# Graph attention kernel, phase A: one group of edges in four gets its column terms from bf16 products instead of gathers

## What is computed

```python
f1 = relu(x[row] @ nb_W[l] + nb_b[l])
f2 = relu(x[col] @ self_W[l] + self_b[l])
h = relu(concatenate([f1, f2], 1) @ att1_W[l] + att1_b[l])
log_alpha = (h @ att2_W[l] + att2_b[l])[:, 0]
mask = clip(sigmoid(log_alpha) * (ZETA - GAMMA) + GAMMA, 0.0, 1.0)
rowsum = segment_sum(mask, row) + 1e-06
d = clip(rowsum ** -0.5, 0.0, 10.0)
vals = mask * d[row] * d[col]
x = segment_sum(vals[:, None] * x[col], row)
out = out + x
```

## Time and profile before

| | |
|---|---|
| median of 3 runs | 12785.2 us (12784.3 to 12812.13) |
| profiled execution: span, first to last instruction | 9111.0 us |
| rest of the median, outside the profiled span | 3674.2 us |
| sort and setup | to about 612 us |
| node phase, each layer | about 55 us |
| phase A, each layer | 2095 to 2100 us |
| rest of a layer (phase B and the node phase behind it) | 693 to 720 us |

### The profile page before, as it was taken

One profiled execution on the slowest core, in us unless ns is written; L12 is line 12 of the kernel. 1 busy time (PEld: TensorE's weight loads), 2 busy tenths in 40 slices (PEclk: granted clock), 3 DMA queues, 4 the chain that ended last, 5 costly groups with the idle time before them and its releaser, 6 DMA issues.

```text
span 9111.0 us, 203370 instructions
## 1 busy us (share of the span) xinstructions
PE 5650.8 (62%) x43467; PEld 5151.5 (57%) x43630; DVE 6736.5 (74%) x29039; ACT 3666.1 (40%) x8663; POOL 5960.7 (65%) x6294
## 2 busy tenths in 40 slices
PE   3135555555558996555555557998555555555996
PEld 1135555545548885555555556887555555555886
DVE  8877777777777877777777777877777777776788
ACT  0013322322227883322322325885322322323886
POOL 0017777777775656777777776665777777776664
PEclk7565555555558996555555557998555555555998
DMA  1014444444456664444444446665444444445665
GB/s 24 0 48 135 132 130 131 132 130 130 133 128 206 213 206 130 132 131 130 132 130 131 132 130 176 210 212 156 132 130 130 133 130 131 132 130 146 213 211 161
DMA packets 1122388, 1272.27 MB, mean 140 GB/s; under 512 B 648596, under 2 KB 652724, under 8 KB 1122356
## 3 DMA queue, kind: packets, MB, share of 16 engines
q1 hardware_dynamic: 922676, 903.51, 32.1%
q0 software_dynamic: 199680, 368.45, 16.7%
HBM read 868.11 MB, written 403.23 MB: 140 GB/s over the span
## 4 chain that ended last, share of the span: by engine, by line
POOL 44%; issue 23%; PE 22%; DVE 8%; DMA 1%; ACT 1%; POOLq 0%; DVEq 0%; ACTq 0%; SPq 0%
POOL got L526 22%; PE bank L552 12%; POOL k_hot L526 11%; POOL g_hot L526 10%; PE bank L685 6%; DVE acc L946 2%; DVE acc L947 2%; PE bank L653 1%; PE bank L690 1%; PE bank L610 1%; PE bank L601 1%; PE bank L576 1%; DMA k_x<-kept_x 1%; DMA k_hot<-qx_table,index 0%; DVE acc L909 0%
## 5 line engine op out<-in xcount | busy, mean ns | idle before, releaser
L653 PE MATMUL bank<-p_all,onehot_t 128*128 x10032 | 2301.5, 424 | 1752.4 <-issue 1731.8
L653 PEld LDWEIGHTS bank<-p_all,onehot_t 128*128 128x128 f32 x10032 | 2186.8, 330 | 1803.4 <-issue 1803.4
L526 POOL DMA_INDIRECT got<-qx_table,index x2496 | 2376.4, 952 | 784.9 <-issue 780.3
L539 POOL DMA_INDIRECT got<-y_table,index x1248 | 1187.3, 951 | 798.8 <-issue 431.5
L798 ACT ACTIVATE small<-small 128x8 f32<-128x8 f32 x624 | 130.2, 209 | 3813.9 <-DVE small L1080 3813.9
L526 POOL DMA_INDIRECT k_hot<-qx_table,index x1248 | 1181.3, 947 | 393.7 <-issue 377.5
L526 POOL DMA_INDIRECT g_hot<-qx_table,index x1248 | 1185.6, 950 | 380.6 <-issue 380.6
L552 PE MATMUL bank<-mask,onehots 128*128 128x3 bf16 x4992 | 669.8, 184 | 986.1 <-DVE mask L1091 986.1
L552 PEld LDWEIGHTS bank<-mask,onehots 128*128 128x128 bf16 x4992 | 516.0, 104 | 1250.7 <-issue 1145.5
L1118 DVE SCALAR_TENSOR_TENSOR p_all<-iota_b,col_hi,bank 128x104 f32<-128x104 bf16 x3768 | 953.9, 317 | 341.5 <-PE bank L685 335.4
L1056 DVE TENSOR_SCALAR onehots<-iota_b,rows_b 128x128 bf16<-128x128 bf16 x5016 | 888.7, 280 | 48.0
(11 more groups left out here) (167 smaller groups left out, 8859.7 us busy)
## 6 DMA issues: line engine op xcount, KB each, us to landing
onehot_t<-look_hot SPq DMA_DIRECT2D x474, 256.0 KB
row_hot<-onehots SPq DMA_DIRECT2D x468, 256.0 KB, 3.6
k_x<-col_rows SPq DMA_DIRECT2D x318, 256.0 KB, 3.6
kept_x<-got SPq DMA_DIRECT2D x312, 256.0 KB
look_hot<-k_x SPq DMA_DIRECT2D x312, 256.0 KB, 2.1
hot_in<-row_hot SPq DMA_DIRECT2D x312, 256.0 KB
k_x<-kept_x SPq DMA_DIRECT2D x312, 256.0 KB
look_new<-row_hot SPq DMA_DIRECT2D x159, 256.0 KB
```

Of the source, the lines that this page charges most:

```text
L526: pool.indirect_dma_start(got[j][:, k, :], None, qx_table, bass.IndirectOffsetOnAxis(ap=index[j][:, k:k + 1], axis=0)).then_inc(a_got[j], 16)
L539: pool.indirect_dma_start(got[j][:, k, 0:HID], None, y_table, bass.IndirectOffsetOnAxis(ap=index[j][:, k:k + 1], axis=0)).then_inc(g_got[j ...
L653: last = mm(bank_p[h][:, k, :], onehot_t[h][:, k, :], p_all[:, ds(ids[k], 1), :].rearrange("p o d -> p (o d)"), start=True, stop=True)
```

## The change

The groups with j = 3 lose their gathers. Their column terms come from PE. For that,

- the sort key's fields are moved (COL_AT, HI_AT), and after the sort the 256 pieces of 1024 edges are ranked by how many runs of equal column block they hold, and moved in DRAM (sorted_keys), so that the groups with the fewest runs become the j = 3 groups; what a j = 3 group needs is then at most SLOTS = 72 products: ROUNDS = 9 rounds of 8;
- nine rounds of max and match_replace per group list the runs, 36 gathers on POOL (line 621 of the new kernel) fetch the lanes, and the lists go to DRAM: slot_words (per product: which block of q, which tile of the group) and slot_lanes;
- the node phase cuts q in three exact bf16 parts, kept in SBUF as q3 (192 columns a block): two more DVE instructions, one on ACT and one on POOL for each of thirteen steps;
- in phase A, SP loads nine broadcasts of 256 KB a quad (slot_in), DVE makes nine one-hots of 128 x 1024 bf16 (build_slots), and PE clears four banks and makes 72 bf16 products of 192 columns into bank_q (column_terms), three rounds each in the steps j = 0, 1 and 2. The row terms of the j = 3 group are added into the same banks, and DVE sums the three parts with one reduction;
- each one-hot of rows is now built once, with one instruction of 128 x 1024, and used for both purposes; block_of is int32 now; the clearing of acc moves from ACT to POOL; the weights are loaded anew for each layer.

The constants and the register sources:

```diff
+    ROUNDS = 9
+    SLOTS = ROUNDS * U
+    PARTS_OF = 3
+    Q_COLS = PARTS_OF * HID
+    OUT_COLS = 256
...
-        block_of = sb("block_of", [1, TILES + AHEAD], mybir.dt.int16)
-
-        spot_of = sb("spot_of", [1, TILES + U], I32)
+        tile_at = sb("tile_at", [64, TILES + AHEAD], I32)
+        block_of, spot_of = tile_at[0:1, :], tile_at[32:33, :]
```

SP and POOL in phase A:

```diff
+                        if j == 0:
+
+                            sp.wait_ge(x_used[0], l * (slots_used(0) * QUADS) + b * slots_used(0))
+                            sp.sem_inc(sp_go, 1)
+                            sp.dma_start(slot_word[0:1, :], slot_words[ds(b, 1), 1, :]).then_inc(w_in, 16)
+                            for r in range(3):
+                                load_slots(b, r, 0 if r == 0 else None)
...
-                    for j in range(4):
-
-                        pool.wait_ge(a_idx[j], l * (QUADS + (j < 3)) + (b + 1))
+                    for j in range(3):
+
+                        pool.wait_ge(a_idx[j], l * (QUADS + 1) + (b + 1))
```

PE in phase A:

```diff
+                def column_terms(b, j):
+
+                    n = l * QUADS + b
...
+                    for r in range(3 * j, 3 * j + 3):
+                        pe.load(q_at + k_at, slot_word[0:1, 2 * U * r:2 * U * (r + 1)])
+                        pe.wait_ge(x_made, n * ROUNDS + (r + 1))
+                        for i in range(U):
+                            of = pe.snap(q_at[i], min_val=0, max_val=(NB - 1) * Q_COLS)
+                            to = pe.snap(k_at[i], min_val=0, max_val=(U - 1) * OUT_COLS)
+                            last = plus(bank_q[:, ds(to, Q_COLS)],
+                                        slot_hot[r % 2][:, i * PARTS:(i + 1) * PARTS],
+                                        q3_flat[:, ds(of, Q_COLS)])
+                        last.then_inc(x_used[r % 2], 1)
...
-                with pe.Fori(0, GROUPS // 2) as b:
-                    for j in range(2):
-                        g = b * 2 + j
-                        row_terms(1 - j, g + 1, a_sum, l * GROUPS + g)
-                        turn_hot(j, g + 2)
-                        at = [pe.snap(r, min_val=0, max_val=BLOCKS - 1) for r in blk[j]]
-                        pe.wait_ge(a_hotb, l * (GROUPS + 1) + (g + 1))
+                with pe.Fori(0, QUADS) as b:
+                    for j in range(4):
+                        g = b * 4 + j
+                        if j == 2:
+                            column_terms(b, j)
+                            row_terms(1, g + 1)
+                        else:
+                            row_terms(1 - j % 2, g + 1, a_sum, l * GROUPS + g)
+                        turn_hot((j + 2) % 4, g + 2)
+                        if j == 0:
+
+                            pe.wait_ge(a_sum, l * GROUPS + g)
+                            for i in range(4):
+                                clear(bank[4 + i])
+                        if j < 2:
+                            column_terms(b, j)
```

DVE in phase A:

```diff
-                def build_hot(to, rows, g, n, free, signal, stored=None):
...
-                    for k in range(U):
-                        last = v.tensor_scalar(to[:, k, :], iota_b[:, :], rows[:, k:k + 1], None, ALU.is_equal)
-                    last.then_inc(signal, 1)
+                def build_hot(j, g, summed_up, stored):
...
+                    build_onehot(hot[j], row_lo[:, ds(g * U, U)]).then_inc(a_hot, 1)
+
+                def build_slots(b, r):
+
+                    h = r % 2
+                    dve.wait_ge(x_in[r % 3], (l * (3 * QUADS) + (b * 3 + (r // 3 + 1))) * 16)
+                    dve.wait_ge(x_used[h], l * (slots_used(h) * QUADS) + (b * slots_used(h) + r // 2))
+                    v.tensor_scalar(slot_hot[h], slot_in[r % 3], part_f[:, :], None, ALU.is_equal).then_inc(x_made, 1)
...
+                        if j < 3:
+                            build_slots(b, 3 * j)
+                            build_slots(b, 3 * j + 1)
+                        build_hot((j + 2) % 4, g + 2, g, b + (j >= 2))
...
+                            v.tensor_reduce(terms, q_parts[:, :, 0:Q_COLS].rearrange("p k (s d) -> p k d s", s=PARTS_OF),
+                                            AX.X, ALU.add).then_inc(a_parts, 1)
...
                         link(v.tensor_reduce(sm[:, 0, :], hidden[h][:, :, :], AX.X, ALU.add), e)
+                        if j < 3:
+                            build_slots(b, 3 * j + 2)
```

More of the change, by code:

```diff
@@ L206, in build @@
         onehots = sb("onehots", [PARTS, 4 * U, PARTS], BF16)
-        hot_a, hot_b = ([onehots[:, h * U:(h + 1) * U, :] for h in (first, first + 1)] for first in (0, 2))
+        hot = [onehots[:, j * U:(j + 1) * U, :] for j in range(4)]
         onehot_t = ring("onehot_t", [PARTS, U, PARTS], F32)
@@ L212, in build @@
                   .rearrange("p (k m) -> p k m", m=PARTS) for c in range(3)]
-        index = [sb(f"index{h}", [PARTS, U], I32) for h in range(4)]
+        index = [sb(f"index{h}", [PARTS, U], I32) for h in range(3)]
         hidden = ring("hidden", [PARTS, U, HID], F32)
@@ L574, in _ @@
                 of = keys[stages_before(n) % 2]
+                if n == TURNS - 1:
+                    pe.wait_ge(s_ranked, 1)
+                    for h in range(2):
+                        last = turn(bank[7][:, h * PARTS:(h + 1) * PARTS], other[:, h * PARTS:(h + 1) * PARTS], ident_f[:, :])
+                    last.then_inc(s_kk, 1)
+                    of = other
+                    pe.wait_ge(s_perm, 16)
+                    pe.wait_ge(s_lo, 1)
                 for c in range(COLS // PARTS):
@@ L790, in make_look @@
                     a.activation(look_new[j], look_new[j], ACT.Relu, bias=one[:, :], scale=-1.0).then_inc(a_look[j], 1)
+                for j in range(4):
+                    act.wait_ge(q_lo[j], stores(l + 1, (0, j)))
                 keep_turned(0, 0, 0)
@@ L985, in _ @@
                     n += 1
-            done, free = keys[n % 2].bitcast(I32), keys[(n + 1) % 2].bitcast(I32)
-            link(v.tensor_scalar(free, done, PARTS - 1, None, ALU.bitwise_and))
-            v.tensor_copy(col_lo, free).then_inc(s_lo, 1)
+            done, moved = sorted_of.bitcast(I32), other.bitcast(I32)
+            own, real, group_key, runs, rank, first, rest, few, kk = (ranks[:, k, :] for k in range(9))
+            link(v.tensor_scalar(moved, done, HI_AT, None, ALU.logical_shift_right))
@@ new lines, in _ @@
+            link(v.memset(run_start.rearrange("p (t e) -> p t e", e=PARTS)[:, :, 0:1], 1.0))
+            link(v.tensor_tensor(run_by, run_val, iota_e, ALU.add))
+            pair = [starts[:, 0:GROUP_EDGES], run_by]
+            link(v.tensor_tensor(pair[0], run_by, run_start, ALU.mult))
+            for r in range(ROUNDS):
+                eight = picks[:, 0, r * U:(r + 1) * U]
+                link(v.max(eight, pair[r % 2]))
+                link(v.match_replace(pair[(r + 1) % 2], eight, pair[r % 2], 0.0))
```

386 lines of the change are left out of this document (291 added, 95 removed).

## The result

The changed kernel takes **13283.7 us** (median of 4 runs, 13279.7 to 13295.4) against 12784.8 us (12775.1 to 12812.1): ratio 1.0385, 95% interval 1.037 to 1.040. It is slower by 499 us. The prediction said 13350 us.

A forecast was written before the change was run, and what follows sets the result against it. POOL's gathers were taken to bound phase A before, PE's sequencer and waits after; phase A +437, setup +100 and node phase +25 sum to 562 us, on 12785 giving 13350 us, range 12450 to 14150.

The forecast's parts named there:

- POOL bounds the kernel before with no slack: Phase A before: 32 gathers a quad at 1.255 us fill its 40.2 us, so POOL is the bound.
- In time that the profile doesn't show; I keep that as it is: Whole kernel: the median lies 3674 us above the profiled span, and this is carried over unchanged.
- A quad of 43 us, +2.8: Phase A after: 44.1 us at 1.2 GHz, 38.7 at 2.4, three parts in four low; against 40.2, +437 us.
- PE's sequencer as the floor: Phase A after: register loads and variable addresses make PE's sequencer need 35.5 us a quad without waits, above POOL's 30.1.
- The waits: Phase A hand-overs between PE and DVE: at 1.2 GHz, waits of 2.6 (j = 0), 1.0 (j = 1), 3.7 us (group 3).
- Setup: Once, before the layers: ranking, scatters, run lists and 36 gathers add 100 us (80 to 140), covered by nothing.
- Node phase: Two more DVE steps of 0.69 us in each of 39 steps: +0.6 us a step, +25 us (0 to 60).
- POOL as the bound: Rival, phase A: PE's path is shorter and POOL stays the bound, 30.1 to 37 us a quad, faster; 12%.
- the fast clock: Rival: PE at 2.4 GHz throughout, 38.7 us a quad, 12676 us; 38 to 41 us a quad has 18%.
- dear loads: Rival, PE's new register loads: 2.1 us each gives 14900 us, 0.26 a value 19000; 12% for all above 47 us.
- The time outside the span growing with the rest: Rival: the median stays 1.40 times the span, so 562 us becomes 562 x 1.40 and the time 13573 us; 8%.
- A quarter of POOL's time idle: Expected sign in phase A after: POOL idles on index for a quarter of the time.

The follow-up runs named there:

- experiment 3: The changed kernel with 2 of 8 gathers a group issued in phase A: 11849.9 us, a quad of 47.9 us.
- experiment 7: The kernel before with 2 of 8 gathers a group issued in phase A: 9054.4 us, a quad of 30.9 us.
- experiment 8: The changed kernel with 2 of 8 gathers in phase A, no nine register loads a quad and fixed product addresses: 10801.6 us.
- (2): The changed kernel with all gathers, without the nine register loads a quad and with fixed addresses in the column products: 12940.2 us.
- The two profiles: The kernel before, unchanged, profiled ahead of the prediction (span 9111 us) and once more afterwards (12819.9 us, span 12818.1).

## Why the prediction was right, and where it was not

The time came within 0.5% and the sign was right. Of the mechanism the longer path of PE and DVE was right; two other steps were wrong, the length of that path and the time outside the span, and nearly cancelled; that the number came so near is luck.

- **POOL bounds the kernel before with no slack** (40.2 us a quad): wrong for the executions that are timed. A quad takes 54.6 us there; POOL's gathers take 40.2 of them, and in the other 14.4 it stands idle. This step failed, because the profile was taken as an execution like the timed ones.
- **"In time that the profile doesn't show; I keep that as it is"**: wrong as a reading. The 3674 us lie inside phases A and B (a layer takes 2838 + 1215 us by the stretches above, and 2100 + 720 in the earlier trace rows; three times the difference is 3699 us). In phase A, three fifths of it, they are waits for held signals; in phase B that is shown for 192 us of 456 a layer. Kept as it is it wasn't either: the held time of a quad fell from 14.4 us (54.6 - 40.2) to 8.9 (56.8 - 47.9).
- **A quad of 43 us, +2.8**: the new quad is 56.8 us, +2.2. The difference was near, the parts were not. The path without holding is 47.9 us (experiment 3), so the predicted 44.1 at 1.2 GHz is 3.8 short, and against 40.2 the change costs 7.7 us a quad, not 2.8. That the held time fell by 5.5 brought it back to 2.2. The old path is 30.9 (experiment 7), which POOL's 40.2 hid in the first profile.
- **PE's sequencer as the floor**: half shown. Its loads and variable addresses are worth 6.7 us a quad on the bare path (experiment 8), 2.2 with the gathers (2), and 41.3 us remain without them. In the kernel as it runs the late signals set the end.
- **Prices**: the load of sixteen int32 was 1.11 us for 0.95 taken; the reduction 1.76 for 1.75; the slot one-hot 0.49 for 0.45. The Trainium skill ("Runtime: NRT & Kernel Launch", Instruction fetch mechanics) would have 3.2 us for the load by its 200 ns a register, a figure that the page gives for registers loaded from HBM (slot_word lies in SBUF); the trace does not agree.
- **The waits**: DVE's were forecast to be longest for x_used of round 0 and a_p of group 3. The first is by far the longest, 13.5 us (median), the second 4.3, and those for x_used of other rounds reach 7.3; 2.6 and 3.7 were worked out as what PE loses there. The size of the first was the holding's: in experiment 3 no wait "remote" is left there.
- **Clock** 0.5 to 0.8: 0.55. **Setup** +100: +108; its terms as listed add up to about 115. **Node phase** +25: +5 in the first layer and +8 in each of the others, 21. **Phase B** 0: 1127 us in both.
- **Rivals**: POOL as the bound and the fast clock were out, and so were dear loads. The time outside the span growing with the rest was out as well; there was no time outside it. The 79 us a quad of the dearest loads is a slip: nine loads of 4.2 for 0.95 us make 43 into 72.
- **A quarter of POOL's time idle**: it is nearly half (24 gathers at 1.255 us are 30.1 of 56.8 us), most of it on index as forecast.

Not tried: another buffer for the third slot, so that DVE needn't wait for round 0 inside the step. It should take away the wait on which the held signal falls, but not the holding.

## What to carry to other kernels

Compare a profile's span with the time of its own execution before anything is summed: where they differ by more than some microseconds, it shows another execution, and its bound may not be the bound. Where GpSimd issues indirect gathers in long rows, let it wait for them every four or eight; such waits made the two kernels here 10 and 13% faster. Look first whether signals do come late: in the first profile of before, with longer rows, they did not. A change that takes work off an engine should be costed against the bare path of the others, measured with that work cut out, since a full engine can hide how short it is (here 30.9 us beneath 40.2).

## What the hardware showed that was not expected

While POOL issues gathers 1.25 us apart with no pause, semaphore signals of the other engines arrive late: DVE's idle time before a step that waits for DVE itself grows from 0.03 us at the first gather of a row of sixteen to 1.22 at the twelfth, and a signal of TensorE came 13 us after the recorded end of its work (3028.2 to 3041.34). With waits of 2.3 to 5.7 us behind every four or eight gathers this is nearly gone in phase A. The Trainium skill ("SBUF — State Buffer", Who interferes with whom) has one case of engines in each other's way, VectorE and GpSimd at a shared port, which blocks instructions. The trace does not bear that out as the cause: DVE's steps still take 0.17 us and the gathers 0.94; only the time between them grows, and ScalarE waits for TensorE, which the page gives ports of their own.

What path the signals share with the gathers stays open, and so does why one execution, the first profile of before, had its gathers back to back and no late signals at all. The two profiles differ in one more thing: of the 19968 landing signals on the semaphore of got[0], sixteen for each of its 1248 gathers, the first has 19907 and the second 1440. The trace doesn't tell whether the others merged on the way or were only not recorded. Every execution whose span is known here was recorded, so a part of the recording itself in the delay isn't ruled out either.

A register load of sixteen int32 on TensorE takes 1.11 us (median; 1.32 in experiment 3), of eight 0.59 and of eight int16 2.1.
